# Two attention layers on one core: a rebuilt opening, and another order of the chunks

## The reference

```python
# layer 0 attention
q = l2norm(q); k = l2norm(k)                      # over all 128 columns of a row
attn = softmax((q/sqrt(D)) @ (k/sqrt(D)) / temperature)
x = layernorm(x + attn @ v @ proj_w.T + proj_b)
x = layernorm(x + int8_quantised_matmul(x, weight_q) * scales + bias)
# layer 1: layernorm and rotary on q and k per head, causal softmax
x = layernorm(x + causal_attention(x))
x = layernorm(x + (silu(x @ wg.T) * (x @ wu.T)) @ wd.T)
```

## Time and profile before

| | us |
|---|---|
| median of 3 runs | 810.11 (810.07 to 810.95) |
| the profiled execution, whole | 810.68 |
| its span | 808.6 |
| PE busy | 791.6 (98%) |
| ACT busy | 767.8 (95%), of it exponentials 745.9 |
| DVE busy | 527.7 (65%) |
| POOL busy | 174.7 (22%) |

### The profile page before, as it was taken

How to read it: one execution, slowest core, us unless ns; L and a number is a source line. 1 busy time by engine, 2 the same in 40 slices (tenths; PEclk the granted TensorE clock), 3 DMA queues, 4 the chain that set the end, 5 groups by cost and what they waited for, 6 DMA issues and landing times.

```text
span 808.6 us, 18428 instructions
## 1 busy us (share of the span) xinstructions
PE 791.6 (98%) x7469; PEld 295.9 (37%) x7469; DVE 527.7 (65%) x1422; ACT 767.8 (95%) x869; POOL 174.7 (22%) x370
## 2 busy tenths in 40 slices
PE   8999999999999999999999999999999999999996
PEld 4333333333333433443333433343333343443444
DVE  4253657758758788687862685766573387787646
ACT  4999999999999999999999999999999999999982
POOL 3111101101102601033100511023300263363220
PEclk9999999999999999999999999999999999999999
DMA  5776232415404711532170431231231231053000
GB/s 148 253 235 208 89 122 82 154 41 183 144 28 157 272 41 40 183 144 93 41 260 27 124 112 42 92 128 44 92 131 51 69 130 54 28 182 120 15 15 16
DMA packets 48553, 88.71 MB, mean 110 GB/s; under 512 B 5200, under 2 KB 14544, under 8 KB 48464
## 3 DMA queue, kind: packets, MB, share of 16 engines
q1 hardware_dynamic: 47696, 85.95, 31.2%
q0 software_dynamic: 288, 1.05, 0.4%
q10 hardware_dynamic: 480, 0.48, 0.2%
HBM read 50.50 MB, written 35.65 MB: 107 GB/s over the span
## 4 chain that ended last, share of the span: by engine, by line
PE 74%; ACT 14%; DVE 7%; issue 3%; POOL 1%; DMA 0%; ACTq 0%; DVEq 0%; POOLq 0%
PE ps L896 36%; PE ps L874 21%; ACT probs L717 13%; PE ps L763 8%; PE ps L752 3%; PE ps L849 2%; DVE th L1282 1%; DVE hT L1283 1%; PE ps L930 1%; PE ps L757 1%; ACT th L677 0%; PE ps L938 0%; DVE gate_sb L1279 0%; POOL v_all L590 0%; PE ps L791 0%
## 5 line engine op out<-in xcount | busy, mean ns | idle before, releaser
L717 ACT ACTIVATE probs<-ps 128x1024 f32<-128x1024 f32 x800 | 745.9, 1057 | 15.3 <-PE ps L874 11.3
L896 PE MATMUL ps<-probs,v_st 128*32 128x512 f32 (+3 forms) x3584 | 425.0, 556 | 3.3 <-issue 1.8
L874 PE MATMUL ps<-q_st,k_st 32*128 32x512 f32 (+3 forms) x1792 | 257.4, 459 | 2.1 <-ACT probs L717 0.9
L874 PEld LDWEIGHTS ps<-q_st,k_st 32*128 32x128 f32 x1792 | 119.6, 182 | 281.8 <-ACT probs L717 226.5
L627 POOL TENSOR_SCALAR_AFFINE_SELECT probs<-probs 128x256 f32<-128x256 f32 x256 | 104.3, 430 | 141.0 <-ACT probs L717 138.9
L896 PEld LDWEIGHTS ps<-probs,v_st 128*32 128x32 f32 x3584 | 79.9, 108 | 110.2 <-issue 80.9
L595 POOL COPY v_st<-v_all 128x256 f32<-128x256 f32 (+1 forms) x65 | 25.6, 402 | 343.3 <-PE ps L896 335.2
L1256 DVE COPY mid_qkv<-ps 128x384 f32<-128x384 f32 x32 | 17.8, 558 | 45.5 <-PE ps L763 43.8
L1137 DVE STREAM_TRANSPOSE sums_t<-ps 128x512 f32<-128x512 f32 x32 | 22.9, 717 | 29.1 <-PE ps L896 29.0
L1287 DVE TENSOR_TENSOR last_y<-ps,last_y 128x128 f32<-128x128 f32 x24 | 7.0, 292 | 42.6 <-PE ps L763 42.6
L849 PE MATMUL ps<-yTp,w_hid 128*128 128x512 f32 x84 | 30.8, 448 | 1.7 <-DVE gate_sb L1279 0.3
(11 more groups left out here) (192 smaller groups left out, 636.2 us busy)
## 6 DMA issues: line engine op xcount, KB each, us to landing
k_st<-parts_scratch SPq DMA_DIRECT2D x46, 512.0 KB, 3.5
parts_scratch<-mid_part SPq DMA_DIRECT2D x34, 512.0 KB, 4.0
q_st<-parts_scratch SPq DMA_DIRECT2D x62, 256.0 KB, 3.9
parts_scratch<-prep_part SPq DMA_DIRECT2D x28, 512.0 KB, 4.3
k_st<-parts_scratch SPq DMA_DIRECT2D x17, 256.0 KB, 2.8
xT<-in_xT SPq DMA_DIRECT2D x8, 256.0 KB, 4.2
x_all<-in_x SPq DMA_DIRECT2D x8, 256.0 KB, 6.6
out<-yo SPq DMA_DIRECT2D x7, 256.0 KB, 2.3
```

The costliest lines, as they stand in the source:

```text
L717: nc.scalar.activation(probs[:, k % PS, :, 0:w], slot(k)[:, :, 0:w], ACT.Exp).then_inc(probs_ready, 1)
L874: last_ = mm(slot(k)[:, e, at:at + n], k_st[row, p % KB, kt * P:(kt + 1) * P], q_st[row, p % KB, lo:HALF], start=True, stop=not shifted)
L896: last_ = mm(acc[HR * h:HR * (h + 1), lo:HALF], v_st[:, p % VB, kt, h, :], probs[:, (2 * s + h // 2) % PS, h % 2, at:at + n], start=FIRST[ ...
```

## The change

Two things are done together.

**The chunk order** is now three chunks of layer 0, then layer 1 and layer 0 in turns. `ORDER` is written anew for it. Two rows of the diff stand for the table:

```diff
-CHUNKS = [(0, 0), (0, 1), (0, 2), (0, 3), (1, 0), (0, 4), (1, 1), (0, 5),
-          (1, 2), (0, 6), (1, 3), (0, 7), (1, 4), (1, 5), (1, 6), (1, 7)]
+CHUNKS = [(0, 0), (0, 1), (0, 2), (1, 0), (0, 3), (1, 1), (0, 4), (1, 2), (0, 5), (1, 3), (0, 6), (1, 4), (0, 7), (1, 5), (1, 6), (1, 7)]
```

**The opening** builds pass 0's operands in place. Chunk 0's q, k and v are projected into banks of their own, DVE takes k's norms with bn_stats while ACT squares q, one tensor_tensor writes the first 32 columns four times over (`first_qk`), PE turns that, and sign and low-half factors per partition (new columns of `w_cols`) make the mixtures directly in `k_st` and `q_st`:

```diff
-        for c in range(2):
-            pe.wait_ge(x_in[c], 16)
+        pe.wait_ge(x_in[0], 16)
+        for n, bank in enumerate((ACC, SIDE, V_BANK)):
             for t in range(TC):
-                mm(ps[:, c * TC + t, 0:3 * C], xT[:, c, t * P:(t + 1) * P], w_qkv[0],
-                   start=True, stop=True).then_inc(head_qkv, 1)
+                last_ = mm(ps[:, bank, t * P:(t + 1) * P], xT[:, 0, t * P:(t + 1) * P], w_qkv[0][:, n * C:(n + 1) * C],
+                           start=True, stop=True)
+            last_.then_inc(head_qkv, 1)
...
+            act.wait_ge(head_qkv, 1)
             for t in range(TC):
-                act.wait_ge(head_qkv, t + 1)
-                square(0, t)
+                square(t, ps[:, ACC, t * P:(t + 1) * P], job["prep"]["st"][:, 0, 2 * t:2 * t + 1])
...
+                if t == HEAD_SQUARES:
                     act.wait_ge(tcol_made, 1)
+                    for u in (1, 0):
+                        act.wait_ge(first_turned, 2 - u)
+                        nc.scalar.activation(first_sign[:, u, :], ps[:, FIRST_BANK[u], :], ACT.Copy,
+                                             scale=(sign_q, sign_k)[u]).then_inc(first_signed, 1)
...
+            for t in range(TC):
+                ch.step(v.bn_stats(bn[:, t, :], by_t(side)[:, t, :]))
+            ch.need()
+            for t in range(TC):
+                ch.step(v.bn_aggr(mv[:, 2 * t:2 * t + 2], bn[:, t, :]))
...
+            roots(0)
+            for u in (1, 0):
+                op = tt(first_qk[:, :, u, :, :], by_t(ps[:, ACC + u, :])[:, :, 0:HR].unsqueeze(3).to_broadcast([P, TC, HR, PRODUCTS]),
+                        per(0, 1)[:, :, u].unsqueeze(2).unsqueeze(3).to_broadcast([P, TC, HR, PRODUCTS]), ALU.mult)
+                op.then_inc(first_scaled, 1)
+            flags(1)
+            for u, dst in ((1, k_st[:, 0, 0:HALF]), (0, q_st[:, 0, :])):
+                dve.wait_ge(first_signed, 2 - u)
+                stt(out=dst, in0=ps[:, FIRST_BANK[u], :], scalar=(low_q, low_k)[u], in1=first_sign[:, u, :].bitcast(F32),
+                    op0=ALU.mult, op1=ALU.add).then_inc(first_made, 1)
```

The ordinary turns and halves of chunk 0 (`head_turn`) now come behind scores 0 to 2; `FIRST_KEYS` gains the unit `firstT`, which makes the second 512 keys of pass 0 in the same way. Only pass 1's rows still come by small DMAs, eight of them, three on POOL's queue:

```diff
+        pool.wait_ge(parts_ready, 1)
+        for y in range(1, PRODUCTS, PARTS):
+            first_rows(pool, 1, 1, k_st, y, low_rows_in)
+        pool.wait_ge(parts_ready, 2)
+        first_rows(pool, 1, 0, q_st, PRODUCTS - 1, low_rows_in)
...
-    WARM = (10, 4, 0, 22, 7)
+    WARM = (8, 3, 8, (4, 5, 7))
...
+        sp.wait_ge(x_in[0], 16)
         for dst, src in ((w_qkv[1], a["w1_qkv"]),
...
             elif what == "ffn":
                 for t in range(TC):
-                    last_ = mm(side[:, t * P:(t + 1) * P], xqT[:, t * P:(t + 1) * P], w_ffn[:], start=True, stop=True)
+                    last_ = quarters(side[:, t * P:(t + 1) * P], xqT[:, t * P:(t + 1) * P], w_ffn[:])
...
-        with sp.If(far_scores > 0):
+        with sp.If(far_scores < 1):
+            steps(False)
+        with sp.Else():
             steps(True)
-        with sp.Else():
-            steps(False)
```

More of the change, by code:

```diff
@@ L846, in stage @@
                 last_ = turn4(lambda t: buffers(name, c)["qk"][:, t, k * C:(k + 1) * C], side, ident)
+            elif what == "firstT":
+                pe.wait_ge(first_scaled, 3)
+                last_ = turn4(lambda t: first_qk[:, t, k, :, :].rearrange("p f y -> p (f y)"), side, ident)
             elif what in ("gate", "up"):
@@ L887, in sums @@
                         pe.wait_ge(sums_turned, p // 2)
+            if not s:
+                pe.wait_ge(parts_ready, 2)
             if tiles_[0][0:2] == (0, TC):
@@ L974, in steps @@
                 for name, c, e, what, k in SIDE_ORDER[s]:
[L975 to L976 removed]
+                    if e == "pe" and not (shifted and (name, c, e, what, k) in FIRST_KEYS):
                         stage(name, c, what, k)
@@ L1258, in read @@
                     got()
+            elif what == "firstT":
+                chain[name].link(ts(first_sign[:, k, :], side, sign_k, None, ALU.mult))
+                stt(out=k_st[:, 0, HALF:S], in0=side, scalar=low_k, in1=first_sign[:, k, :].bitcast(F32),
+                    op0=ALU.mult, op1=ALU.add).then_inc(side_read, 1)
             elif what == "qkT":
@@ L1352, in _ @@
         counted_consts = cc.n
-        with dve.If(far_scores > 0):
-            steps(True)
+        with dve.If(far_scores < 1):
+            steps(False)
         for n, ch in chain.items():
```

279 lines of the change are left out of this document (157 added, 122 removed).

## The result

| | before | after |
|---|---|---|
| median of 20 runs each, us | 810.70 (810.07 to 811.22) | 811.96 (810.31 to 816.06) |
| ratio after / before, 95% interval | | 1.0023 (1.0014 to 1.0031) |
| profiled execution, whole / span | 810.68 / 808.6 | 811.34 / 809.5 |

A forecast was written before the change was run, and what follows sets the result against it. ACT's exponentials, 0.925 us apart, were taken as the clock, with PE nearly full. Opening -4.1, rows +0.2, moved units -1.55 and last parts +1.5 sum to -3.95: 810.11 to 806.2 us, range 802.8 to 808.9.

The forecast's parts named there:

- The opening: Kernel start to the first exponential: it would start at 15.7 in place of 19.83, -4.1 us.
- Step 2: Opening's projections, twelve matmuls of 128 columns: q ready 6.4, k 7.1, v 7.75, chunk 1's four end at 9.1.
- the flag and the branch: Opening, after PE's matmuls on zeros: the flag's load and the branch cost at most 0.63 us, to 15.4.
- Behind the opening: Pass 1's late rows, before exponential 8: PE stands 1 us, ACT 0 to 0.6; +0.2 us.
- The estimate of 0.6: Stall behind the opening if POOL's DMAs give their first byte 0.4 us later than SP's: 0.6 us.
- The moved units: Same units carried by other pairs: layer 0's pairs +1.15, (1,5) -2.70; together -1.55 us, bounds -3.5 and +1.5.
- The last parts: Chunk 7's q halves 2.0 to 2.8 us later, PE stands at step 374: +1.5 us, bounds 0 and 3.
- The ffn in quarters: int8 product as 16 matmuls for 4: +0.17 us of PE per chunk, up to 1.4 in all, taken as 0.
- The turned branches: Every engine branches while its queue has something running: taken as 0, at most a few tenths.
- the end still 22.9: Sign to look for: the end's code is unchanged, so it keeps its 22.86 us.
- D: Rival: PE's wait at step 374 becomes a chain, chunk 6's feed-forward holds `end()`: +2.55 us, 812.7; chance 0.04.
- the 0.57 taken off for the median: The profiled execution, 810.68, was 0.57 above the median, so the forecast started from a median of 810.11.

The follow-up runs named there:

- the last run: New opening, order of before with the slot after it mended, DVE's branch turned, SP's not; ffn matmuls whole in place of quarters: 808.53 us, 0.9974 to the kernel before.

## Why the prediction was wrong

- **The opening, -4.1: right in sum, not in each step.** 3.86 measured, scores at 15.43 for 15.0 to 15.4. Step 2 was mis-sized: a projection stands in the rows as two matmuls, so 5.63/16 = 0.35 is half of one. Chunk 1's four took 2.75 us for 1.4 and ended at 11.4 for 9.1, v was ready at 8.8 for 7.75. It cost only 0.6 us at the scalings, since the weights landed 0.45 sooner and ACT and DVE need only q and k; and the scores still came near 15.4 since the flag and the branch, charged with 0.6 behind the matmuls on zeros, cost next to nothing. Part of the fit is luck. The same opening in other executions starts its exponential between 14.67 and 16.04.
- **Behind the opening, +0.2: too small.** 0.94, and 0.66 to 1.18 elsewhere. I took 2.2 us to landing for all rows; the last took 3.7. The estimate of 0.6, from the first-byte figure for POOL's DMAs in the Trainium skill, DMA: Bandwidth & Descriptors, was nearer, but not for its reason: SP's own last row took as long as POOL's (3.73 and 3.64), and with no row on POOL two of q's still took 3.1.
- **The moved units, -1.55: wrong sign.** (1,5) gained 1.96 of the 2.70. The layer 0 pairs cost nothing more (-0.2 for +1.15). But I held the pairs (1,0) to (1,4) at nothing, and they took 3.3. (1,1) has 14 units before and 15 after, and 1.70 of its new idle time is one slot with two fills: counting units per pair could not see it. (The text counts four light pairs of layer 0 before; they are five, and the sum is made with five.)
- **The last parts, +1.5: right in kind, too large here.** In the profiled execution PE waited 0.56 and the two pairs (1,6) and (1,7) idle 0.07 more; in four relatives PE waited 1.35 to 1.73 and (1,6) idles 1.4 to 1.7 for 0.23.
- **The ffn in quarters, 0: right**, as far as the last run can tell.
- **"The turned branches: every engine branches while its queue has something running; taken as 0": the step that failed first.** It looked at the jump into the steps and not at the one out of them. The two cost 2.09 us at "the end still 22.9", which was 24.95, of it 1.8 for SP's. On DVE the same edit saves a stall that the new opening lays bare, which I had not seen either.

The failed steps are two: this one, taken as 0 for 2.1, and the moved units, -1.55 for +1.1 in ACT's waits. In numbers, 4.85 us between the span forecast and the span measured: 0.24 opening, 0.74 rows, 1.78 for units and last parts together (1.73 for -0.05), 2.09 end. None of the rivals had the end in it; D, the only slower one, gave 812.7, near the 811.96 measured, by a mechanism that did not occur. The medians (806.2 and 811.96) lie 0.9 us further apart than the spans, mainly for two reasons: the 0.57 taken off for the median was chance of three runs (over 20 runs the median before is 810.70, the profiled execution 810.68), and the changed kernel's median lies 0.6 above its profiled execution.

Open: the runs of the changed kernel spread from 810.31 to 816.06, those of before by 1.2 us. The five others with the new order and its last parts in place also spread, by 2.7 to 4.5 us; those with the order of before by 0.8 to 2.4. The record has one hint, the mean granted clock of each run. In the changed kernel it is 0.996 to 0.999 for the thirteen runs up to 812.78, and 0.993 to 0.996 for the seven above. In four profiles of other variants the clock fell to 0.50 for 3.4 us in mid-stream, five times in all, each time after PE had stood 1.7 to 3.8 us; one such fall takes 0.002 off the mean (an estimate, 3.4 x 0.5 / 810). So stands of PE that are followed by one or two falls would fit the long runs. That is not shown: no profile caught a long run of the changed kernel, and two relatives have runs of 814.26 and 816.24 with a clock of 0.998 and 0.997.

## What to carry to other kernels

A branch has two jumps: ask for each engine which of the two has cover, and put the path that is taken so that it falls through where there is none. They may be different sides on different engines. In an order of slots, count fills of one bank per slot and not only units per stage, and look at the queue of the engine that empties the banks: where DVE is full, PE cannot be sped up. A wait marked "issue" need not be idle issue time; look in the kernel for what the instruction waits for, and for what ended just before it. A stand of one engine can cost more than its length, if the clock falls behind it. When a stage is relieved, look at every stage that has no slack, not only at the two that were talked about. Split a package: here the opening with DVE's turned branch, in the order of before, is worth 0.36%, the order that came with it costs 0.46% by itself, and SP's turned branch most of 0.18%.
